# Small-head attention: the row maxima carried into one row per head of q's stack by DMA

## The reference, cut to what matters

```python
def _L1_attn_ref(x, Wq, Wk, Wv, Wo):     # x: (4, 1024, 128), H = 16 heads of hd = 8
    q = (x @ Wq.T).reshape(B, S, H, hd)  # k, v likewise
    q = q * cos - jnp.roll(q, 1, axis=-1) * sin   # k likewise
    scores = jnp.einsum('bhqd,bhkd->bhqk', q, k) / math.sqrt(hd)
    attn = jax.nn.softmax(scores, axis=-1)
    ctx = jnp.einsum('bhqk,bhkd->bhqd', attn, v)
    return ctx @ Wo.T
```

## Time and profile before

| | |
|---|---|
| median of 3 runs | 4496.72 us (4495.04 to 4506.08) |
| the profiled execution | 4475.59 us |
| its span in the profile | 4473.8 us |
| busy TensorE, VectorE, ScalarE, GpSimd | 89%, 76%, 65%, 50% |
| units of the changed stage | about 2087 to 2868 us of the span |

### The profile page before, as it was taken

One profiled execution on the slowest core, in us unless ns is written; L12 is line 12 of the kernel. 1 busy time (PEld: TensorE's weight loads), 2 busy tenths in 40 slices (PEclk: granted clock), 3 DMA queues, 4 the chain that ended last, 5 costly groups with the idle time before them and its releaser, 6 DMA issues. The chain is left out here.

```text
span 4473.8 us, 88017 instructions
## 1 busy us (share of the span) xinstructions
PE 3975.3 (89%) x34586; PEld 2227.3 (50%) x34588; DVE 3385.5 (76%) x4741; ACT 2913.3 (65%) x4403; POOL 2240.4 (50%) x1443
## 2 busy tenths in 40 slices
PE   6999999999999979996877777899788877999999
PEld 3666667666666654442111211245677543444443
DVE  6888888888884547767898899565877657878887
ACT  3777777777776449982677777685556644555555
POOL 2888888888886013331121210172566554555555
PEclk7999999999999989996899999898899988999999
DMA  3212212212210011100121100142000224454544
GB/s 84 59 40 59 58 38 59 59 40 58 58 35 16 1 49 48 71 24 29 50 74 43 40 27 16 57 149 72 11 13 15 75 83 115 113 124 116 120 113 108
DMA packets 113913, 270.28 MB, mean 60 GB/s; under 512 B 24276, under 2 KB 36308, under 8 KB 111004
## 3 DMA queue, kind: packets, MB, share of 16 engines
q1 hardware_dynamic: 98084, 223.86, 18.7%
q0 software_dynamic: 15424, 40.89, 2.6%
HBM read 178.10 MB, written 50.81 MB: 51 GB/s over the span
## 5 line engine op out<-in xcount | busy, mean ns | idle before, releaser
L522 POOL TENSOR_TENSOR a_prob_low<-a_prob_whole,a_prob_high 128x1024 f16<-128x1024 f32 x512 | 1085.0, 2131 | 276.7 <-ACT a_prob_high L412 275.6
L496 DVE TENSOR_REDUCE a_part_max<-a_top 128x2 f32<-128x1024 f32 x512 | 626.2, 1223 | 218.7 <-PE a_top L323 212.6
L409 ACT ACTIVATE a_prob_whole<-a_score 128x1024 f32<-128x1024 f32 x512 | 525.2, 1026 | 332.5 <-PE a_score L312 320.5
L976 ACT ACTIVATE a_prob<-a_score 128x512 f32<-128x512 f32 x1024 | 533.1, 603 | 255.9 <-PE a_score L915 255.8
L1009 DVE TENSOR_REDUCE a_part_max<-a_side 128x2 f32<-128x1024 f32 x512 | 595.2, 1220 | 68.3 <-PE a_side L886 68.3
L412 ACT ACTIVATE a_prob_high<-a_score 128x1024 f16<-128x1024 f32 x512 | 521.8, 1019 | 0.0
L311 PE MATMUL a_score<-a_qa,a_ka 128*128 128x256 f16 x2048 | 476.8, 273 | 0.0
L312 PE MATMUL a_score<-a_qb,a_kb 128*128 128x256 f16 x2048 | 476.5, 273 | 0.0
L2185 POOL TENSOR_TENSOR m_lows<-m_scaled,m_high 128x512 f16<-128x512 f32 x264 | 311.2, 1183 | 323.8 <-ACT m_high L2146 322.2
L378 PE MATMUL a_o_ps<-a_v,a_prob_high 128*128 128x65 f16 x4096 | 428.2, 193 | 6.2 <-POOL a_prob_low L522 3.4
L380 PE MATMUL a_o_ps<-a_v,a_prob_high 128*128 128x64 f16 x4096 | 427.0, 194 | 0.0
(11 more groups left out here) (477 smaller groups left out, 10147.8 us busy)
## 6 DMA issues: line engine op xcount, KB each, us to landing
m_gate<-gates SPq DMA_DIRECT2D x264, 256.0 KB, 5.2
a_ka<-a_nat_high_k SPq DMA_DIRECT2D x128, 128.0 KB, 2.4
e_gate<-gates SPq DMA_DIRECT2D x8, 2048.0 KB, 7.2
slots<-in_slots SPq DMA_DIRECT2D x19, 520.0 KB, 4.2
a_qa<-a_nat_high_q SPq DMA_DIRECT2D x64, 128.0 KB, 2.4
a_qa<-a_nat_low_q SPq DMA_DIRECT2D x64, 128.0 KB, 2.4
a_qb<-a_nat_high_q SPq DMA_DIRECT2D x64, 128.0 KB, 2.4
a_kb<-a_nat_low_k SPq DMA_DIRECT2D x64, 128.0 KB, 2.4
```

The source lines that it names most:

```text
L409: eng.activation(prob_whole[:, e % RING, :, :, :], score[:, e % 2, :, :, :], ACT.Exp, scale=scale)
L496: eng.tensor_reduce(part_max[:, i, c, :, qt % 4], top[:, :, :], AX.X, ALU.max).then_inc(max_done, 1)
L522: eng.tensor_tensor(prob_low[:, e % RING, :, :, :], prob_whole[:, e % RING, :, :, :], prob_high[:, e % RING, :, :, :], ALU.subtract).then_ ...
L976: eng.activation(prob[:, e % RING, h, :], score[:, step % SLOTS, :], ACT.Exp).then_inc(exp_done, 1)
```

## The change

The maxima of a half keep four columns per head in place of 32, so `row_max` has 16 columns and the turn gives 16 rows (4 heads times 4 query tiles). VectorE negates these rows into a 16-bit tile `shift` in one operation. SyncE stores this tile to DRAM, waits for it, and loads for each head its four rows as one row of 512 queries into partition 32h + 24 of q's stack. The other seven spare rows stay zero. The first score of a half waits for these four loads. The maxima of a unit and its shifts stand one event earlier than before (but for unit 0's), the first two loads of stacks are issued at the start, load n + 1 stands between the two shifts of unit n, and the store of the next batch follows the third unit's second shift. The mask `less1`, its load and the memset are gone.

```diff
@@ small_attention: timeline()
-                    put(start - 2, "shift", n, 0)
+                    put(start - 3, "shift", n, 0)
                 for m in range(16):
-                    put(start - 11 + 8 * i + m // 2 if n or not i else m // 2, "max", n, 16 * i + m)
+                    put(start - 12 + 8 * i + m // 2 if n or not i else m // 2, "max", n, 16 * i + m)
...
-            put(start + (6 if n else 7), "shift", n, 1)
+            put(start + (5 if n else 7), "shift", n, 1)
@@ tiles
-        part_max = pl.sb("part_max", [P, 2, 2, HEADS, 32])
-        row_max = pl.sb("row_max", [P, 2, P])
+        part_max = pl.sb("part_max", [P, 2, 2, HEADS, 4])
+        row_max = pl.sb("row_max", [P, 2, 4 * HEADS])
+        shift = pl.sb("shift", [4 * HEADS, 2, P], F16)
+        shifts = nc.dram_tensor(f"{stage}_shifts", (2, 4 * HEADS, P), F16, kind="Internal").ap()
+        shift_out = [pl.sem(f"shift_out{i}") for i in range(2)]
+        shift_in = [pl.sem(f"shift_in{i}") for i in range(2)]
@@ sync
+                def turned_shift(n, i):
+                    eng.wait_ge(side_freed, nth["shift", n, i] + 1)
+                    if n:
+                        eng.wait_ge(shift_in[i], 16 * HEADS * n)
+                    eng.dma_start(shifts[i, :, :], shift[:, i, :]).then_inc(shift_out[i], 16)
+                    eng.wait_ge(shift_out[i], 16 * (n + 1))
+                    for h in range(HEADS):
+                        row = 32 * h + 3 * DH
+                        eng.dma_start(qa[row:row + 1, n % 2, i * BANK:(i + 1) * BANK],
+                                      shifts[i, 4 * h:4 * h + 4, :].rearrange("t q -> (t q)").unsqueeze(0)).then_inc(shift_in[i], 16)
+
                 store(0)
+                load(0)
+                load(1)
                 for n in range(units):
-                    if n % GROUPS == 3 and n // GROUPS + 1 < B:
+                    turned_shift(n, 0)
+                    if 0 < n < units - 1:
+                        load(n + 1)
+                    turned_shift(n, 1)
+                    if n % GROUPS == 2 and n // GROUPS + 1 < B:
                         store(n // GROUPS + 1)
-                    load(n)
@@ tensor
-                        mm = eng.transpose(side[:, 0, 0:P], row_max[:, job[2], :], ident[:, :])
+                        mm = eng.transpose(side[0:4 * HEADS, 0, 0:P], row_max[:, job[2], :], ident[:, :])
...
                     if first and k % kts == 0:
-                        eng.wait_ge(side_freed, nth["shift", n, k // kts] + 1)
+                        eng.wait_ge(shift_in[k // kts], 16 * HEADS * (n + 1))
@@ vector
-                eng.memset(part_max[:, :, :, :, :], 0.0).then_inc(filled, 1)
...
-                        op = eng.tensor_reduce(part_max[:, qt // 4, c, 2 * pair:2 * pair + 2, 24 + qt], side, AX.X, ALU.max)
+                        op = eng.tensor_reduce(part_max[:, qt // 4, c, 2 * pair:2 * pair + 2, qt % 4], side, AX.X, ALU.max)
                     elif what == "shift":
-                        for qt in range(4 * job[2], 4 * job[2] + 4):
-                            here = qa[:, n % 2, qt * P:(qt + 1) * P]
-                            op = eng.scalar_tensor_tensor(out=here, in0=side[:, 0, 0:P], scalar=less[:, qt:qt + 1], in1=here,
-                                                          op0=ALU.mult, op1=ALU.add)
+                        if n:
+                            eng.wait_ge(shift_out[job[2]], 16 * n)
+                        op = eng.tensor_scalar(shift[:, job[2], :], side[0:4 * HEADS, 0, 0:P], -1.0, None, ALU.mult)
```

More of the change, by code:

```diff
@@ L712, in vector_rest, with small_attention @@
                 self.then(eng, eng.tensor_copy(self.slot_of[:, j, :], self.where[:, :]))
-def small_attention(nc, stage, res_t, xn_t, w, wo, ident, less, rope, w_moe_d, b_moe_d, split_d, split_out, route,
+def small_attention(nc, stage, res_t, xn_t, w, wo, ident, rope, w_moe_d, b_moe_d, split_d, split_out, route,
                     rows, slot_of, slots_d, cleared, cleared_count, scattered, w_e_in, b_e_in):
@@ L832, in _ @@
                 pl.clear_before(eng)
-                eng.wait_ge(filled, 3)
+                eng.wait_ge(filled, 2)
                 def store(b):
@@ L3041, in program @@
                 ("avg", "bias0", "ident", "rowmask0", "w_b0", "bias_b0", "w_g0", "b_g0", "tri", "dest2", "base2", "sort1", "w_g1", "w_qkv1",
-                 "w_o1", "less1", "rope", "bias2", "w_g2", "mask2", "w_route")}
+                 "w_o1", "rope", "bias2", "w_g2", "mask2", "w_route")}
         avg_in = pl.sem("avg_in")
@@ L3077, in program @@
             with nc.sbuf_tensor("rows1", [P, 2, NT, P + 2], F32) as rows, nc.sbuf_tensor("slot_of1", [P, 2, NT], U32) as slot_of:
-                small_attention(nc, "a1", res_t, xn_t, kept["w_qkv1"], kept["w_o1"], kept["ident"], kept["less1"], kept["rope"], d["w_moe1"], d["b_moe1"], split_d, split_out,
+                small_attention(nc, "a1", res_t, xn_t, kept["w_qkv1"], kept["w_o1"], kept["ident"], kept["rope"], d["w_moe1"], d["b_moe1"], split_d, split_out,
                                 (kept["w_g1"], kept["tri"], kept["ident"], kept["dest2"], None, rows, slot_of, 1e-9, kept["sort1"], w_row),
@@ L3125, in lay_out @@
     rope[:, :, 0], rope[:, :, 1] = table / np.float32(np.sqrt(8.0)), table
-    less1 = np.where(p % 32 - 24 == j[:, 0:8], -1.0, 0.0).astype(np.float32)
     def narrow(w):
@@ L3161, in lay_out @@
         "ident": np.eye(P, dtype=np.float32), "tri": (p <= j).astype(np.float32),
-        "rowmask0": rowmask0, "less1": less1,
+        "rowmask0": rowmask0,
         "bias0": a["L0_attn_bo"].reshape(P, 1), "w_qkv0": w_qkv0,
```

## The result

| | before | after |
|---|---|---|
| median of 7 runs each, us | 4500.4 | 4521.9 |
| profiled execution, us | 4475.6 | 4512.8 |
| its span, us | 4473.8 | 4510.9 |

After to before is 1.0044, 95% interval 1.0032 to 1.0056: 20 us slower. The same kernel measured again, against runs of before on the same chip, gave 1.0026 (1.0014 to 1.0037), 12 us slower. The forecast was 14 us slower, 4511 us. The ratios in this text leave out three executions that took far longer than the others of their kernels: one of ten without the transfers (5207 us) and two of ten with unit 0 covered (4716 and 4719 us).

A forecast was written before the change was run, and what follows sets the result against it. The prediction took the loop of TensorE and ScalarE to bound ordinary events, VectorE just following. Its terms, -6.5 - 3 + 7 + 9 + 1.5 + 6 = +14 us, added to the 4496.7 us median gave 4511 us, range 4480 to 4542.

The forecast's parts named there:

- the second halves' miss of 7: First scores of second halves: a 5.6 us trip exceeds the 5.15 us cover by 0.45 us, 15 times, +7 us.
- the 6 for meetings with GpSimd's transfers: Second halves' round trips: three of eighteen GpSimd weight transfers meet them, 2 us each, +6 us (0 to 12).
- rival 3: Round trip shorter than its cover and meeting nothing: +1 us, 4498 us; chance 0.08.
- The bound: Ordinary events of the stage: set by the loop of TensorE and ScalarE, VectorE only just following; a shift costs 0.58 or 0.45 us.
- Rival 1: VectorE is the bound, so all 30 us of its relief count: -20 us, 4477 us; chance 0.17.
- The gain of 9.5 us: VectorE's relief on the path: 6.5 us from the shifts' additions and 3 us from the smaller merge.
- The trip's length: From VectorE's negation through DRAM store and four loads to the first score: 5.6 us, low end 4.5, high end 6.9.
- The covers: Time from VectorE's start to the waiting score, with the turn one event earlier: first halves 7.4 us, second halves 5.15 us.
- Unit 0, 9 us: Unit 0's two first scores lack cover and wait for the round trip, 2 x 4.4 us: +9 us (7 to 13).
- The clock stood among the rivals: TensorE's half-clock stretches move or two are added through unit 0's new waits: +15 us, 4526 us; chance 0.08.
- The 1.5 us for unit 0's event with four maxima: Unit 1's maxima begin one event earlier beside unit 0's, giving one more four-maxima event: +1.5 us (0 to 2.4).

The follow-up runs named there:

- without the transfers: The changed kernel without its transfers through DRAM, the first scores waiting for the negation alone and the maxima not subtracted; ratio to before 1.0015, stage 776.8 us.
- unit 0 covered: The changed kernel with unit 0's second-half maxima packed four to an event and its second shift in event 4; ratio to before 1.0018, stage 805.4 us.
- the relief alone: The kernel before with the small VectorE operations, its events kept, nothing transferred and the maxima not subtracted; ratio to before 0.9996, stage 773.4 us.
- three stores: The changed kernel with the store to DRAM made three times in a row, each waited for; one run, span 4629.1 us, stage 903.0 us.
- late maxima: The changed kernel with maxima and first shift at their old events, only the second shift one event earlier; ratio to before 1.0031, stage 790.4 us.

## Why the prediction was right

The sign and the size were right: +14 us forecast, +20 and +12 measured. That the sum came out well was luck. 13 of its 14 us, the second halves' miss of 7 and the 6 for meetings with GpSimd's transfers, came to nothing; the trip went as in rival 3 (shorter than the cover, +1 us, 4498), which had 0.08. A cost of about the same size that the sum did not have, that of the moved events, stood in their place. Step by step:

- **The bound.** Right. A clean half is set by the loop of TensorE and ScalarE; of VectorE's 30 us of relief 0.64 us a unit, 10 us, reach the path. Rival 1, with 4477 us, is excluded by the run with the relief alone, and ordinary pairs stayed at 5.0 us.
- **The gain of 9.5 us.** Right in size for the path: 0.64 us a unit is 10 us over 16 units, and the stage was 10 to 14 us shorter. It was not spread evenly, 0.59 us in first halves and 0.06 in second ones. The total has none of it.
- **The moved events.** This term was missing. I put the earlier turn down as 2.5 us more cover and gave the move no price. It costs 1.10 us a unit, 18 us over 16 units at most, and 1.0026 as measured alone. In the clean halves this is what ate the gain.
- **The trip's length.** 5.6 us forecast, 3.8 measured. The store was taken at 2.0 and took 1.35 to the first load's issue; three issues at 1.5 took 0.87; the landing at 1.7 took 1.26. Each of these three was below its nearest row, and the whole below the low end of 4.5: small transfers are cheaper than any row.
- **The covers.** Right. 5.15 us for second halves by the earlier trace rows; the changed kernel has 5.2, and with three stores it is used up.
- **Second halves' miss, 7 us.** Wrong, 0, since the trip was shorter. For the same reason the 6 us for meetings with GpSimd's transfers came to nothing: three stores did take 2.3 to 3.5 us, the longest (issue at 2628.67, loads at 2632.14) in a first half, and the covers bore them. The mechanism itself is real: with late maxima and their shorter cover such stores made scores wait.
- **Unit 0, 9 us.** The place was right: 7.4 us of waits, 14.5 us with the clock behind them against the kernel without the trip, and 5 to 11 us against the two profiles of before, which is what the sum was about. The clock stood among the rivals, at 0.08, as an addition to the forecast. It belonged into this term. The 1.5 us for unit 0's event with four maxima can't be told apart in these.
- **The rule of the Trainium skill** (TensorE: Matmul & The Clock Gate, section on HAM oscillation), that gaps in TensorE's work bring its clock to half: the earlier trace rows couldn't show it, since the gap, 1.25 us at 2177.3, stands ahead of that window. The second wait of unit 0 and the run with three stores agree with it (0.50 behind the wait, 0.80 in the mean), and so do 30 of the 31 falls counted above; the 36 idle times without a fall show that a gap of 1 to 2 us alone doesn't decide it. The figure of about 2 us for a transfer (DMA: Bandwidth & Descriptors, anatomy of one DMA) was too long for these, 1.3 us; the page gives it for the software path.

Against the kernel before, the traces add up as follows. Behind the first four halves, with the shortest of its profiles for each half, the kernel before takes 621 us and the changed one 624: +3. The first four halves give +5 to +11, and the tail +1 in the second profiles (+7 in the first). Halves with projections and output work moved both ways (26.8 to 25.6 and to 25.2 us, but 25.3 to 27.4). The rest of the scatter is half-clock stretches, up to 13 us a profile in either kernel, so the +12 to +20 of the totals can't be split more finely.

## What to carry to other kernels

A masked or padded operation on an engine that is 90% busy was worth no more here than the excess that its events show over plain ones (0.64 us of 1.03 a unit); read that from the distances of a repeated instruction, not from its duration. Price a moved step in a tightly ordered loop even when nothing is added to it, by asking which long event it now stands next to. Before sending something on a round trip through DRAM, measure the time between producer and consumer; if it is too short anywhere, or too short for the slowest store, count the clock behind the wait beside the wait. And look what else an operation will now run beside: beside GpSimd's work one merge took 2.03 us in place of 0.18.

## What the runs showed of the hardware

- A 4 KB store from 16 partitions, and 1 KB loads back, land in 1.3 us in the middle and 3.5 at worst; issuing such a load costs 0.25 us where one of a 64 KB stack costs 0.61.
- VectorE's merge, otherwise 0.18 us (0.29 with 128 columns), took 0.7 to 2.1 us in 18 cases over the 14 profiles. Each of them began beside an operation of GpSimd on its weights and ended within 0.2 us of that operation's end.
- 30 of 31 falls of TensorE's clock from 1.00 to 0.50 came within some 2 us of an idle time of TensorE of 1.1 to 2.7 us; 36 idle times of 1.0 to 2.2 us had no fall behind them. 17 us at half clock cost 6.5 us. In one execution with seven waits of 0.2 to 1.6 us in 490 us the mean clock there was 0.80, where it is 1.00 without them.
- With unused matmuls in the tail the clock was 1.00 where it had been 0.52, and the stretch was 4 us shorter for them.
